# One layer of a four-layer fused kernel: the recurrence's sums by accumulating DMA, and two Hadamard products in whole fp32

## The reference

```python
def bi_wkv(r, k, v, w, u, time_emb):        # called with k = v = fside
    decay = exp(-exp(w)) * (0.5 + 0.5 * tf)
    ek = exp(minimum(k, 30)); ekv = ek * v
    # a scan over time, forward (nf, df) and reversed (nb, db), of ekv and of ek
    euk = exp(minimum(u + k, 30))
    num = nf + nb - ekv + euk * v
    den = df + db - ek + euk
    return sigmoid(r) * (num / maximum(den, 1e-8)) * (0.8 + 0.2 * tf)

def hbitlinear(x, w):                        # 8-bit activations, ternary weights
    xh = fwht(x)                             # Walsh-Hadamard transform over the last dimension
    return einsum('bsh,oh->bso', act_quant(xh), weight_quant(w))

def L1_ffn(z, w_up, w_down):                 # 512 -> 1024 -> 512
    return hbitlinear(square(relu(hbitlinear(z, w_up))), w_down)
```

## Time and profile before

| what | value |
|---|---|
| median of 3 runs | 1774.15 us (1770.31 to 1774.62) |
| profiled execution, its own time | 1784.06 us |
| its span | 1782.1 us |
| layer 1 in it | 558.2 to 833.9 us |
| TensorE busy over the whole span | 1542.7 us (87%) |
| VectorE, ScalarE, GpSimd | 1135.3 (64%), 987.7 (55%), 336.4 us (19%) |

### The profile page before, as it was taken

One profiled execution on the slowest core, in us unless ns is written; L12 is line 12 of the kernel. 1 busy time (PEld: TensorE's weight loads), 2 busy tenths in 40 slices (PEclk: granted clock), 3 DMA queues, 4 the chain that ended last, 5 costly groups with the idle time before them and its releaser, 6 DMA issues. The chain is left out here.

```text
span 1782.1 us, 19975 instructions
## 1 busy us (share of the span) xinstructions
PE 1542.7 (87%) x6541; PEld 995.6 (56%) x6574; DVE 1135.3 (64%) x1806; ACT 987.7 (55%) x1312; POOL 336.4 (19%) x251
## 2 busy tenths in 40 slices
PE   5677587789985999997469999579999999999997
PEld 2222234444443666665434444268888888888886
DVE  7899488899996999996548787745322222222222
ACT  6765588889993999995238777534321221221210
POOL 0000011111210000000614233451231221221211
PEclk9898789999997999998779999879999999999999
DMA  7764632312202543332955454371011101001001
GB/s 282 264 218 160 226 127 84 101 64 68 70 26 67 177 148 125 108 105 102 360 186 189 137 183 144 139 275 40 1 36 36 36 1 36 36 1 36 1 20 75
DMA packets 100808, 199.82 MB, mean 112 GB/s; under 512 B 11492, under 2 KB 28388, under 8 KB 96996
## 3 DMA queue, kind: packets, MB, share of 16 engines
q1 hardware_dynamic: 95012, 180.72, 29.8%
q0 software_dynamic: 5120, 16.78, 2.6%
q10 hardware_dynamic: 576, 1.05, 0.2%
HBM read 139.79 MB, written 58.72 MB: 111 GB/s over the span
## 5 line engine op out<-in xcount | busy, mean ns | idle before, releaser
L2380 ACT ACTIVATE ffn_h<-ffn_pg,ffn_gate_chunk 128x512 f32<-128x512 f32 x64 | 44.0, 688 | 324.4 <-PE ffn_pg L2457 275.5
L2543 DVE SCALAR_TENSOR_TENSOR ffn_h<-ffn_pu,ffn_up_scale,ffn_h 128x512 f32<-128x512 f32 x64 | 48.1, 751 | 231.6 <-PE ffn_pu L2457 231.5
L2553 DVE SCALAR_TENSOR_TENSOR x<-ffn_po,ffn_out_scale,x 128x512 f32<-128x512 f32 x128 | 87.3, 745 | 149.1 <-PE ffn_po L2476 149.1
L2431 POOL TENSOR_TENSOR ffn_hl<-ffn_h,ffn_hh 128x512 fp32r<-128x512 f32 x64 | 82.5, 1289 | 413.0 <-ACT ffn_hh L2387 413.0
L961 POOL TENSOR_TENSOR l_rr<-l_rr,constants 128x1 f32<-128x1 f32 x32 | 28.9, 902 | 488.0 <-DVE l_rr L988 488.0
L2476 PE MATMUL ffn_po<-ffn_hh,ffn_wh 128*128 128x512 f32 x256 | 101.2, 395 | 3.5 <-DVE x L2553 2.9
L2457 PE MATMUL ffn_pg<-zhi,ffn_wh 128*128 128x512 f32 x256 | 101.6, 397 | 0.0
L2457 PE MATMUL ffn_pg<-zhi,ffn_wl 128*128 128x512 f32 x256 | 101.2, 395 | 0.0
L2457 PE MATMUL ffn_pu<-zhi,ffn_wh 128*128 128x512 f32 x256 | 101.1, 395 | 0.0
L2457 PE MATMUL ffn_pu<-zhi,ffn_wl 128*128 128x512 f32 x256 | 101.1, 395 | 0.0
L2457 PE MATMUL ffn_pu<-zlo,ffn_wh 128*128 128x512 f32 x256 | 101.1, 395 | 0.0
(11 more groups left out here) (348 smaller groups left out, 4082.7 us busy)
## 6 DMA issues: line engine op xcount, KB each, us to landing
wkv_k<-in_fside SPq DMA_DIRECT2D x64, 256.0 KB, 3.9
ratio<-wkv_fn SPq DMA_DIRECT2D x64, 256.0 KB, 2.3
wkv_ek<-exp_k SPq DMA_DIRECT2D x48, 256.0 KB, 3.1
wkv_ekv<-exp_k_times_v SPq DMA_DIRECT2D x48, 256.0 KB, 3.8
moe_zt<-tokens_by_slot SPq DMA_DIRECT2D x39, 256.0 KB, 2.9
expert_out<-moe_eo SPq DMA_DIRECT2D x39, 256.0 KB, 2.0
ffn_raw<-in_gated SPq DMA_DIRECT2D x8, 1024.0 KB
x<-in_x SPq DMA_DIRECT2D x4, 1024.0 KB, 7.2
```

The lines of the kernel that those rows point to most:

```text
L2380: eng.activation(hf[t][:, :], p_g[t][:, :], ACT.Silu, scale=scale).then_inc(*E(f"silu{t}").inc)
L2431: eng.tensor_tensor(hl[t][slot % 2][:, :], hf[t][:, :], hh[t][slot % 2][:, :].bitcast(F32), ALU.subtract).then_inc(*E(f"hl{t}").inc)
L2543: eng.scalar_tensor_tensor(hf[t][:, :], p_u[t][:, :], scale, hf[t][:, :], ALU.mult, ALU.mult).then_inc(*E(f"h{t}").inc)
L2553: last = eng.scalar_tensor_tensor(x[:, o, :], p_o[:, o, :], out_s[:, o:o + 1], x[:, o, :], ALU.mult, ALU.add)
```

## The change

All of it is in layer 1.

- The sums of the recurrence leave TensorE. GpSimd issues four accumulating DMAs per unit, each 128 x 512 fp32 (256 KB) from SBUF to SBUF: the later scan onto the forward one for the denominator (`add_later_d`) and the numerator (`add_later_n`), then the exponential onto the denominator (`add_now_d`) and its product with k onto the numerator (`add_now_n`). The PSUM bank goes, and so does `take_num`. `take_den` reads SBUF.
- z and the down weights are no longer split. TensorE multiplies them as whole fp32 tiles: four products for z, one for the weights (class `WholeTransform`, which `front` uses already). Two copies on ScalarE (L1289, L208) and two subtractions on VectorE (L1418, L212) go.
- The lists of all four engines are in a new order. `exps` moves on ScalarE from lag 1, behind the reciprocal, to lag 0, ahead of relu. `take_den`, `ln` and `recip_exp` follow each other at the end of a step. `newton` and `quotient` move forward on VectorE. SP loads k one step later in its own list and stores the quotient two steps later.

```diff
+    def add_later_d(self, eng, i, p):
+        eng.wait_ge(*self.E("scan_d").at(i))
+        eng.wait_ge(*self.E("ends").at(min(i, self.slots - 1)))
+        eng.dma_start(self.fd[p][:, :], self.bd[p][:, :], accum_op=ALU.add).then_inc(*self.added["both"][p].inc)
+
+    def add_now_d(self, eng, i, p):
+        eng.wait_ge(*self.done("both", i))
+        eng.wait_ge(*self.E("exps").at(i))
+        eng.dma_start(self.fd[p][:, :], self.eu[p][:, :], accum_op=ALU.add).then_inc(*self.added["den"][p].inc)
...
-                for k in range(CT):
-                    for t, part in enumerate((zh, zl)):
-                        last = eng.matmul(p_z[:, :], part[p][:, k * P:(k + 1) * P],
-                                          hadamard_row(k),
-                                          start=(k + t == 0), stop=(k == CT - 1 and t == 1))
+                for k in range(CT):
+                    last = eng.matmul(p_z[:, :], z[p][:, k * P:(k + 1) * P], hadamard_row(k).bitcast(F32),
+                                      start=k == 0, stop=k == CT - 1)
...
+        @block.gpsimd
+        def _(eng):
+            for j in range(TILES + 1):
+                for i in due(j, 1, TILES):
+                    w.add_later_d(eng, i, i % w.slots)
+                for i in due(j, 1, TILES):
+                    w.add_later_n(eng, i, i % w.slots)
+                for i in due(j, 1, TILES):
+                    w.add_now_d(eng, i, i % w.slots)
+                for i in due(j, 1, TILES):
+                    w.add_now_n(eng, i, i % w.slots)
...
@@ scalar
-                for i in due(j, 1, TILES):
-                    w.exps(eng, i, i % w.slots)
...
+                for i in due(j, 0, TILES):
+                    w.exps(eng, i, i % w.slots)
                 for i in due(j, 1, TILES):
                     relu_h(i, i % 2)
...
-                    w.take_num(eng, i, i % w.slots)
+                    w.take_den(eng, i, i % w.slots)
+                for i in due(j, 1, TILES):
+                    w.ln(eng, i, i % w.slots)
+                for i in due(j, 1, TILES):
+                    w.recip_exp(eng, i, i % w.slots)
```

More of the change, by code:

```diff
@@ L183, in hadamard_blocks @@
     return built, k
[L186 to L233, removed]
 class WholeTransform:
@@ L296, in __init__ @@
     def __init__(self, core, scope, c, d, out, layer, slots, gate=None, preloads=(), banks=(),
-                 first=0, count=UNITS, tiles=None):
+                 first=0, count=UNITS, tiles=None, added=()):
         self.preloads, self.layer, self.c, self.banks = preloads, layer, c, banks
@@ L309, in __init__ @@
         self.sent = core.dma_event(self.tag + "stored", slots)
+        self.added = {n: core.queue_event(self.tag + n + "_added", slots) for n in added}
         self.e = {}
@@ L334, in cap @@
         if i >= self.slots:
-            eng.wait_ge(*self.E("den").at(i - self.slots))
+            eng.wait_ge(*self.done("den", i - self.slots))
             eng.wait_ge(*self.E("newton").at(i - self.slots))
@@ L441, in den_on_tensor @@
         eng.wait_ge(*self.E("ends").at(min(i, self.slots - 1)))
-        eng.wait_ge(*self.E("scan_d").at(i))
+        eng.wait_ge(*(self.done("both", i) if "both" in self.added else self.E("scan_d").at(i)))
         if i >= 1:
-            eng.wait_ge(*self.E("num_out" if len(self.banks) == 1 else "den_out").at(i - 1))
-        for t, part in enumerate((self.eu, self.fd, self.bd)):
-            last = eng.matmul(bank[:, :], self.c["ident"][:, :], part[p][:, :], start=t == 0, stop=t == 2)
+            eng.wait_ge(*self.E("num_out" if len(self.banks) == 1 and "num" not in self.added else "den_out").at(i - 1))
+        parts = (self.eu, self.fd) if "both" in self.added else (self.eu, self.fd, self.bd)
+        for t, part in enumerate(parts):
+            last = eng.matmul(bank[:, :], self.c["ident"][:, :], part[p][:, :], start=t == 0, stop=part is parts[-1])
         last.then_inc(*self.E("den").inc)
@@ L459, in num_on_tensor, with add_later_n, add_now_n @@
         last.then_inc(*self.E("num").inc)
+    def add_later_d(self, eng, i, p):
[6 more added lines that the diff above has]
+        eng.dma_start(self.fd[p][:, :], self.eu[p][:, :], accum_op=ALU.add).then_inc(*self.added["den"][p].inc)
+    def add_later_n(self, eng, i, p):
+        eng.wait_ge(*self.E("scan_n").at(i))
+        eng.wait_ge(*self.E("ends").at(min(i, self.slots - 1)))
+        eng.dma_start(self.fn[p][:, :], self.bn[p][:, :], accum_op=ALU.add).then_inc(*self.added["later"][p].inc)
+    def add_now_n(self, eng, i, p):
+        eng.wait_ge(*self.done("later", i))
+        eng.wait_ge(*self.E("euv").at(i))
+        eng.dma_start(self.fn[p][:, :], self.k[p][:, :], accum_op=ALU.add).then_inc(*self.added["num"][p].inc)
     def set_ends(self, eng):
@@ L531, in quotient @@
         eng.wait_ge(*self.E("newton").at(i))
-        eng.wait_ge(*self.E("num_out" if self.banks else "num").at(i))
+        eng.wait_ge(*(self.E("num_out").at(i) if self.banks and "num" not in self.added else self.done("num", i)))
         eng.scalar_tensor_tensor(fn, fn, self.neg_gain[:, ds(i, 1)], fd, ALU.mult, ALU.mult).then_inc(*self.E("ratio").inc)
@@ L1264, in _ @@
                     cols_of_q2(i, i % 2)
-                for i in due(j, 1, TILES):
-                    w.den_on_tensor(eng, i, i % w.slots)
+                for i in due(j, 2, TILES):
+                    dt.product(eng, i, i % 2)
                 for i in due(j, 4, TILES):
@@ L1394, in sums_and_differences, with differences @@
                     eng.wait_ge(*E("hl").at(i - 2))
-                first, second = h[p][:, 0:FF1 // 2], h[p][:, FF1 // 2:]
+                first, second = halves(p)
                 eng.tensor_tensor(sums[p][:, 0:FF1 // 2], first, second, ALU.add).then_inc(*E("sum").inc)
+            def differences(i, p):
+                eng.wait_ge(*E("h").at(i))
+                if i >= 2:
+                    eng.wait_ge(*E("hl").at(i - 2))
+                first, second = halves(p)
                 eng.tensor_tensor(sums[p][:, FF1 // 2:], first, second, ALU.subtract).then_inc(*E("difference").inc)
```

108 lines of the change are left out of this document (44 added, 64 removed).

## The result

| | us, median | runs | ratio to before, 95% interval |
|---|---|---|---|
| before | 1773.04 | 4 (1770.31 to 1774.62) | |
| after | 1794.99 | 4 (1794.37 to 1798.2) | 1.0123 [1.0103, 1.0142] |

The change makes the kernel 22 us slower. The profiled execution of after took 1794.37 us. That of before was itself some 11 us above its median, and the excess lies mostly outside layer 1: there its trace has 1506 us, where the eleven other traces of this document have 1495 to 1503 for the same work. So the totals of the two traces don't show where the 22 us are. Layer 1 alone does: from the end of layer 0 to its last residual it takes 294.9 us after (554.44 to 849.31) against 275.7 before, 19 more.

The account below looks back on a forecast made before the run. TensorE's list was taken to bound layer 1 at 15.96 us a step. Fourteen steps of 15.75 plus 14.7 made 0.9 us on, 2 off at the start: about -1 from 1774.15, so 1773 us, range 1760 to 1790.

Parts of the forecast that it names:

- What bounds before: Layer 1 before the change: TensorE never stops, its list alone is the 15.96 us step; VectorE and ScalarE wait.
- TensorE's list: Layer 1 step: 5.2 us off for identity products, 1.6 and 0.2 on for whole products, 15.96 to 12.6 us.
- VectorE 13.8, ScalarE 14.0 to 14.4: Work per layer 1 step after the change: VectorE from 15.15 us, ScalarE from 14.5, its 14.4 including waits between instructions.
- The loop at 15.7 to 15.8: Layer 1, split of h to next split through ScalarE, TensorE and VectorE: 15.7 to 15.8 us a step against 15.96.
- The first rival: The loop over TensorE doesn't bind in layer 1: steps of 15.2 us or less, 1756 to 1765 us; chance 0.27.
- The adds hidden: Accumulating DMAs in layer 1: each add takes about 5 us to land, and 8.3 us each are hidden.
- from 5 to 6 us: GpSimd's issues held up by VectorE's port lock: five delays at most lengthen an add this much, under 8.3.
- The steps are at the full clock in both: Layer 1 steps before and after: full granted clock, so the forecast difference of about -1 us carries over to the median.
- the second rival: TensorE's clock halves behind its idle time in layer 1: 1.3 us a step, 1791, or 1782 every second step; chance 0.18.
- The start 2 us earlier: Start of layer 1: z's product starts first, so the first split of h comes 2 to 3 us earlier, from 0 to 4.
- 14 steps of 15.75: Layer 1's 15 steps: fourteen at this one length plus a last of 14.7, 235.2 us against 234.3.
- A wait that I didn't count, on SP's queue: Named way to be wrong: an uncounted wait appears, above all on SP's queue; no size given.

Follow-up runs that it names:

- e8: The kernel before, with only z and the down weights' tile as whole fp32 products, sums left on TensorE: 1801.77 us, ratio to before 1.0159.
- e9: e5 with `exps` moved on ScalarE behind the exponential of the reciprocal, two table loads a step instead of three: 1790.47 us, ratio to before 1.0068.
- e4: The changed kernel with eight unneeded filler products a step, and on ScalarE `round1` and the weights' copy ahead of the gate: 1782.07 us, ratio to before 1.0062.
- e3: The changed kernel with each accumulating DMA adding only 16 of 512 columns: 1790.08 us, ratio to before 1.01.
- e6: The changed kernel with lists of ScalarE, VectorE and SP reordered and four filler products ahead of h's product: 1754.04 us, ratio to before 0.9888.
- e5: e2 with SP issuing the 1 MB weight loads behind the quotient's store instead of ahead of it: 1779.54 us, ratio to before 1.0032.
- e10: e5 with one filler product a step instead of four: 1793.14 us, ratio to before 1.0088.
- e2: The changed kernel with four unneeded bf16 products of 512 columns a step in front of TensorE's gap: 1783.6 us, ratio to before 1.0064.
- e7: e6 without its filler products: 1759.53 us, ratio to before 0.9917.

## Why the prediction was wrong

Forecast 1773 us, range 1760 to 1790; measured 1795, outside.

- *What bounds before: right. TensorE's list: somewhat short.* e8's list grew by 1.98 us a step for 1.8 predicted. In the changed kernel TensorE is busy 13.37 us in a step at full clock (85%), where I had 12.6 (80%): the sum was short by 0.8, without effect, as TensorE has idle time there.
- *VectorE 13.8, ScalarE 14.0 to 14.4: right*, 13.95 and 14.4.
- *The loop at 15.7 to 15.8: right at full clock*, 15.77, with the waits that were named: 1.21 us in front of the low part of h, and in full-clock steps 0.39 for `round1`, 0.47 in front of the maximum and 1.23 in front of `exps`. The loop over `round1`, maximum and `exps` was read correctly, and e9 confirms that the third load costs nothing in it. The first rival, a shorter loop, is not there: its terms add up to 15.1 and not 15.2, and e4, which should have reached it, stayed at 15.88.
- *The adds hidden: right in steady steps.* Estimate 5 us from issue to landing, measured 3.3 to 6.4, under the 8.3 allowed. As to the engines' time, 7.9% less 2.6% of the span over 64 adds is 1.48 us of all 16 engines each, twice the 0.72 of a gather; in 600 to 820 us, where GpSimd's queue has only adds, it is 1.47 for 256 KB against 0.85 for as much of SP's plain transfers, most of which go to or come from HBM (worked out from packets, MB and share of the 220 us below). The Trainium skill, Collectives: The Full Stack, section "The bandwidth ceiling: the fold count and why AG ≠ RS ≠ AR", has it for collectives that an adding step reads two sources where a copy reads one and runs at half the rate. The trace agrees roughly, with a factor of 1.7 to 2.0; no run has a plain copy from SBUF to SBUF to compare with. The delay that I feared for GpSimd's issues beside VectorE was small: 1.2 us at most instead of 0.86. The line "from 5 to 6 us" for five such delays doesn't follow from its own terms, and nothing hangs on it.

```profile
q1 hardware_dynamic: 16883, 24.63, 36.1%
q0 software_dynamic: 7776, 14.16, 36.0%
```

- *The step that failed: "The steps are at the full clock in both".* It is the second rival, to which I gave 0.18. Its price, 1.3 us for a step, was near the measured 1.03 to 1.05; its frequency was the open term, and eleven of the 15 steps have it, not every second. I had two rows of idle times of 2.40 us with opposite outcomes, for a single gap each. But here the gap comes back in step after step, so that none of them lowers the clock was unlikely, and the rival deserved more than the forecast. The rival's own 1791 was also too low, since it priced only the steady steps. The Trainium skill has a warning in TensorE: Matmul & The Clock Gate, section "A second HAM failure mode: psum-queue depth-cycling": in another kernel, short and frequent idling between groups of products made the clock swing. The trace agrees, with 1.97 us in a step of 15.77.
- *The start 2 us earlier: wrong.* From the end of layer 0 to the first split it takes 26.7 us instead of 25.7, with `take_den`'s wait of 2.4 for the add in it. The adds are needed sooner there than in a steady step. But that isn't the whole of it: in e3, where the wait is 0.7, the first split comes only 0.3 us earlier. With the old lists and whole products (e8) it comes after 23.3 us, with the lists of e6 after 23.5. So the 2 us are to be had, and it is the changed kernel's order that spends them, by `take_den`, logarithm and exponential ahead of the first split or by something else in it; no run tells which.
- *14 steps of 15.75: wrong for the first two even with the clock mended.* In e5 they take 17.75 and 16.81 us at clock 0.81 and 0.90, in before 14.64 and 14.62 at 1.00 (the earlier trace rows have only the sum of all steps). I had one length for all 14. The end from the last split, which I took as unchanged, grew from 15.8 to 19.7 us, and its length goes with its clock: 19.7 at 0.74, 17.6 at 0.90 (e5), 15.8 at 1.00 (e10).
- *A wait that I didn't count, on SP's queue*: named as a way to be wrong, and there: the store behind the megabyte, e5. It is worth 4 us in e2; in the changed kernel itself its two waits are 2.8 us together.

The sum for layer 1 in the traces: 14.2 us in the 15 steps, 4.0 at the end, 0.9 at the start, 19.1 in all. Against the forecast's own terms the 15 steps are 13.3 over: 9.0 in the third to the fourteenth (8.4 of it the clock in eight steps, the rest mostly the late store), 2.5 in the first two, 1.7 in the last. The start is 3.0 over and the end 4.0. The rest up to 22 is not located: it is less than the traces differ by outside layer 1.

With the clock held in the steady steps and the store moved (e5), 5.9 us over before remain. In its trace layer 1 is 6.7 us longer: the twelve steady steps are 2.3 us shorter than in before, and the first two 5.3, the last 1.4, the start 0.5 and the end 1.9 us longer.

## What to carry to other kernels

- Time taken off a saturated TensorE comes back as idle time. If it lies in one piece in each step, price the clock for every step, and for the start and the end as well. A few products that nobody needs tell within one run whether it is the clock.
- An engine's list shortened is not a step shortened. The same work took 15.77 us in one order and 14.52 in another, with one table load less. The new order takes the reciprocal out of the chain that ran in series with the split and TensorE; that this is what gained is argued from the lists, since e6 changed three of them at once, but e9 shows that it wasn't the load. A change of resources is worth testing with the lists laid out for it.
- A store that is waited for must not stand behind a large load on its queue; look at how soon one follows the other, and where each buffer's release hangs, when a lag is changed.

## What was not expected of the hardware

- A gap of 1.97 or 1.75 us in each step of about 16 us brought the clock down in about two steps of three; 1.11 us in 15.77, 1.26 in 15.92 (e9) and 1.40 in 14.51 (e7), never in the steady steps. Two steps at the same gap differ, so a single step tells nothing.
- Added work made the kernel faster: 4 bf16 products of 512 columns a step, 0.9 us, took some 11 us off.
- Accumulating DMAs of 256 KB inside SBUF landed in 3.3 to 6.4 us (medians; up to 7.0 in e6, at a DMA share of 0.81 to 0.88) and cost 1.7 to 2 times the engine time of plain transfers. No compute engine waited for one in steady steps.
- A store of 256 KB issued some 2 us behind a load of 1 MB on the same queue landed in 8.8 to 9.6 us (the changed kernel and e2), ahead of it in 4.2 to 5.1 (e5). In before, with no adds about and 12.6 us behind it, it took 2.1.
